# A nine-tap convolution computed with five products for three outputs instead of four for two

## What is computed

```python
sh = conv1d_same(xt, sh_w1, sh_b1)      # (B, 128, T) -> (B, 512, T), 9 taps
sh = jax.nn.silu(sh)
sh = conv1d_same(sh, sh_w2, sh_b2)      # 512 -> 128, 1 tap
...
z = residual + y + sh                   # y: the sum of the chosen experts
return (z - mu) * jax.lax.rsqrt(var + 1e-05) * ln_g + ln_b
```

## Time and profile before

| | us |
|---|---|
| median of 3 runs | 1534.27 |
| the profiled execution | 1544.43 |
| its span, first to last instruction | 1542.6 |
| TensorE busy (x10360 matmul records) | 1305.9 (85%) |
| VectorE busy | 1003.6 (65%) |
| GpSimd busy | 699.3 (45%) |
| ScalarE busy | 644.9 (42%) |
| convolution products (L1133), busy | 261.6, 1536 records |

### The profile page before, as it was taken

How to read it: one execution, slowest core, us unless ns; L and a number is a source line. 1 busy time by engine, 2 the same in 40 slices (tenths; PEclk the granted TensorE clock), 3 DMA queues, 4 the chain that set the end, 5 groups by cost and what they waited for, 6 DMA issues and landing times.

```text
span 1542.6 us, 33397 instructions
## 1 busy us (share of the span) xinstructions
PE 1305.9 (85%) x10360; PEld 1103.2 (72%) x10361; DVE 1003.6 (65%) x3235; ACT 644.9 (42%) x1610; POOL 699.3 (45%) x1055
## 2 busy tenths in 40 slices
PE   6696777787899937778899899988998989999974
PEld 3464646564899935556788778876887989999953
DVE  4467768665466656757863786467663628989946
ACT  1346272523122204335335453445334436666623
POOL 0112556444688853133531444242614526777732
PEclk9697989898999978989999899999998999999987
DMA  6000400003588840010010001000100237777725
GB/s 191 4 21 6 111 27 22 25 21 95 161 266 256 263 170 1 2 42 1 24 61 0 2 14 58 14 1 1 43 1 8 95 97 191 196 194 198 196 88 161
DMA packets 102202, 128.46 MB, mean 83 GB/s; under 512 B 21015, under 2 KB 61181, under 8 KB 101842
## 3 DMA queue, kind: packets, MB, share of 16 engines
q1 hardware_dynamic: 88786, 102.36, 23.1%
q0 software_dynamic: 13312, 24.74, 4.8%
HBM read 96.13 MB, written 34.94 MB: 85 GB/s over the span
## 4 chain that ended last, share of the span: by engine, by line
PE 60%; DVE 15%; issue 7%; DVEq 6%; POOL 5%; ACT 4%; DMA 2%; POOLq 0%; SPq 0%; ACTq 0%
PE psum L980 12%; PE psum L1133 11%; PE psum L989 9%; DVE work L1554 3%; PE psum L1142 3%; PE psum L1047 2%; POOL rows_in L2130 2%; PE psum L1094 2%; PE psum L1072 2%; PE psum L794 2%; PE psum L1191 2%; PE psum L969 2%; PE psum L1018 2%; DVE stats L1537 2%; PE psum L1067 1%
## 5 line engine op out<-in xcount | busy, mean ns | idle before, releaser
L1133 PE MATMUL psum<-NT,wreg 128*128 128x182 f32 (+1 forms) x1536 | 261.6, 326 | 10.2 <-ACT pack L1434 5.1
L1133 PEld LDWEIGHTS psum<-NT,wreg 128*128 128x128 f32 x1536 | 247.9, 192 | 18.9 <-ACT pack L1434 5.9
L2162 POOL DMA_INDIRECT rows_out<-work,expert_row_kept x208 | 206.2, 992 | 79.6 <-issue 41.1
L980 PE MATMUL psum<-work 128*128 128x128 f32 x1664 | 222.7, 277 | 0.9 <-ACT work L1336 0.9
L980 PEld LDWEIGHTS psum<-work 128*128 128x128 f32 x1664 | 203.9, 193 | 1.7 <-issue 0.9
L2111 POOL TENSOR_TENSOR rstd<-var_eps,pack 128x6 f32<-128x6 f32 x40 | 56.5, 1415 | 215.0 <-DVE var_eps L1544 214.9
L1329 ACT ACTIVATE work<-psum,work 128x128 f32<-128x128 f32 x416 | 118.6, 368 | 64.4 <-PE psum L980 64.3
L1876 DVE SCALAR_TENSOR_TENSOR work<-psum,work 128x128 f32<-128x128 f32 x416 | 117.1, 344 | 7.7
L794 PE MATMUL psum<-pack,work 128*128 128x128 f32 (+2 forms) x288 | 51.4, 336 | 82.0 <-DVE work L1554 75.5
L1885 DVE TENSOR_SCALAR work<-psum,expert_row_kept 128x128 f32<-128x128 f32 x208 | 72.8, 350 | 71.8 <-PE psum L969 36.6
L2130 POOL DMA_INDIRECT rows_in<-N,slot_now x96 | 100.5, 1046 | 28.6 <-issue 28.4
(11 more groups left out here) (364 smaller groups left out, 2894.3 us busy)
## 6 DMA issues: line engine op xcount, KB each, us to landing
work<-w_and_b SPq DMA_DIRECT2D x104, 258.0 KB
work<-in_ew SPq DMA_DIRECT2D x104, 256.0 KB
work<-rows_in SPq DMA_DIRECT2D x208, 65.0 KB
work<-rows_out SPq DMA_DIRECT2D x32, 384.0 KB, 4.2
rows_out<-work,expert_row_kept POOLq DMA_INDIRECT x208
work<-in_xT SPq DMA_DIRECT2D x8, 375.0 KB, 3.0
w_and_b<-in_ew SPq DMA_DIRECT2D x1, 2560.0 KB
out<-H SPq DMA_DIRECT2D x8, 320.0 KB
```

The lines of the kernel that those rows point to most:

```text
L980: r_ = mm(v.ps1[:, c * P:(c + 1) * P], v.w1[:, c * P:(c + 1) * P], v.xT, start=True, stop=True)
L1133: r = mm(bank[:, half * HALF_PAIRS:half * HALF_PAIRS + p1 - p0], weights[:, m * P:(m + 1) * P], product_input(name, g, k, p0, p1), start=( ...
L2162: G.indirect_dma_start(rows_out[m], bass.IndirectOffsetOnAxis(ap=v.dest, axis=0), v.y, None, bounds_check=last, oob_is_err=False).then_inc ...
```

## The change

The convolution now makes three outputs from five products (`CONV_POINTS`). A unit (k, m) is a whole sequence of lane k, 250 triples of outputs (`TRIPLES`), for 128 hidden features; there are 8 units per iteration. A unit has three parts: `p12` (6 products), `p03` (6) and `p4` (3). All parts, and `rows`, alternate between the two PSUM banks. Only `p12` has two SBUF buffers; `p03` and `p4` have one. VectorE combines with seven instructions. `turn` now has twelve GpSimd instructions in four steps with a drain between them. The weights of points 1, 2 and 3 are made by VectorE in the first iteration of the mixer, with five instructions over 1536 columns (`conv_w0` to `conv_w2`), stored to DRAM, and loaded when the first experts are done. Two of the four hidden blocks now lie in the first rows of `H`, which are saved to DRAM before and restored at the end.

```diff
-        FILL = [3, 1, 0, 0, 0, 0, 1, 0] + [0.5, 0.5] * TILES + [3.5, 2, 1.5, 1, 0.5]
+        FILL = [3, 1, 0, 0, 0, 0, 1, 0] + [0.5, 0.5] * TILES + [3.5, 2.5, 2, 1, 0]
...
+            for t in range(3):
+                sp.dma_start(raw_taps[:, t].rearrange("p (g c) -> p g c", g=3),
+                             d["conv1"].rearrange("p (g t c) -> p g t c", g=3, t=3)[:, :, t, :]).then_inc(conv_taps_in, 16)
...
+            sp.wait_ge(conv_made, 1)
+            sp.dma_start(conv_made_dram, raw_taps.rearrange("p t c -> p (t c)")).then_inc(conv_made_out, 16)
             with sp.Fori(1, ITERS) as i:
...
-            for name, dst in (("conv1", conv1), ("conv2", conv2)):
-                sp.dma_start(dst, d[name]).then_inc(conv_in, 16)
+            for t, x in ((0, 0), (2, 4)):
+                sp.dma_start(conv_w[:, x], d["conv1"].rearrange("p (g t c) -> p g t c", g=3, t=3)[:, :, t, :]).then_inc(conv_in, 16)
+            sp.dma_start(conv2, d["conv2"]).then_inc(conv_in, 16)
+            sp.wait_ge(conv_made_out, 16)
+            sp.dma_start(conv_w[:, 1:4].rearrange("p x g c -> p (x g c)"), conv_made_dram).then_inc(conv_in, 16)
...
+            sp.wait_ge(first_rows_final, 1)
+            sp.dma_start(first_rows_dram, first_rows).then_inc(first_rows_out, 16)
...
+            sp.dma_start(first_rows, first_rows_dram).then_inc(first_rows_back, 16)
...
+                    for half, x in enumerate(POINTS[what]):
                         for g in range(3):
+                            r = mm(bank[:, half * TRIPLES:(half + 1) * TRIPLES], conv_w[:, MADE[x], g, k_cols(m)], turned(k)[:, x, g:g + TRIPLES],
+                                   start=(g == 0), stop=(g == 2))
...
+                bk, bm, bi = unit_before(k, m, i, 2 if what == "p12" else 1)
+                e.wait_ge(dve_conv_done, dve_conv.at("conv", f"y{bm}_{bk}", 0, bi))
+                dst = {"p12": conv_p12[u % 2], "p03": conv_p03, "p4": conv_p4}[what]
...
-                V.tensor_tensor(conv_sum[:, 0:n_], b, c, ALU.add)
-                V.tensor_tensor(b, b, c, ALU.subtract)
+                V.scalar_tensor_tensor(conv_sum, p1, 3.0, p2, ALU.mult, ALU.add)
+                V.scalar_tensor_tensor(p2, p1, -3.0, p2, ALU.mult, ALU.add)
+                V.scalar_tensor_tensor(p0, p0, 3.0, p3, ALU.mult, ALU.add)
+                V.scalar_tensor_tensor(conv_p4, conv_p4, 1.5, p3, ALU.mult, ALU.add)
                 e.drain()
...
+                V.tensor_tensor(y[:, 0], p0, conv_sum, ALU.subtract)
+                V.scalar_tensor_tensor(y[:, 1], p3, 2.0, p2, ALU.mult, ALU.add)
+                V.scalar_tensor_tensor(y[:, 2], conv_p4, 4.0, conv_sum, ALU.mult, ALU.subtract
...
             def attention(i, first):
-                if not first:
-                    turn(1, i - 1)
...
                 turn(0, i)
+                for k in range(LANES):
+                    add_ln_b(k, i, first)
+                turn(1, i)
                 add_b_sh2(0, i)
```

More of the change, by code:

```diff
@@ L50 @@
 KTAPS = 9
+TRIPLES = (L + 2) // 3
+TURNED = TRIPLES + 2
 EPS = 1e-5
@@ L456, in run @@
                         continue
-                    if chain == "scatter":
+                    if chain == "conv_w":
+                        steps[step]()
+                    elif chain == "scatter":
                         steps[step](int(pair[0]) if pair else i - 2)
@@ L546, in audio_tower @@
         UNITS = 2 * LANES
-        HALF_PAIRS = SPAN[0][1] // 2
         pe_conv_done, act_conv_done, dve_conv_done = sem("pe_conv_done"), sem("act_conv_done"), sem("dve_conv_done")
-        UNIT = [(q, m) for q in range(UNITS) for m in range(4)]
+        UNIT = [(k, m) for k in range(LANES) for m in range(4)]
+        POINTS = {"p12": (1, 2), "p03": (0, 3), "p4": (4,)}
+        MADE = {0: 0, 1: 2, 2: 3, 3: 1, 4: 4}
         PARTS = []
-        for u, (q, m) in enumerate(UNIT):
-            PARTS.append(("bc", q, m))
-            if m == 1 and q > 0:
-                PARTS.append(("rows", q - 1, 0))
-            PARTS.append(("ad", q, m))
@@ L563, in audio_tower @@
-        dve_conv = Steps({"conv": (ITERS, 1, [f"y{m}_{q}" for q, m in UNIT])})
+        for k, m in UNIT:
+            PARTS.append(("p12", k, m))
+            if m == 1 and k > 0:
+                PARTS += [("rows", 2 * k - 2, 0), ("rows", 2 * k - 1, 0)]
+            PARTS += [("p03", k, m), ("p4", k, m)]
+        CONV_END = [("last", LANES - 1, 3), ("rows", UNITS - 2, 0), ("rows", UNITS - 1, 0)]
+        COST = {"p12": 6, "p03": 6, "p4": 3, "rows": 4}
+        FILLS = [f"{x}{m}_{k}" for x, k, m in PARTS + CONV_END if x != "last"]
@@ L584, in interleaved @@
                 reached += FILL[x // LANES]
-                while conv and n * sum(FILL) * LANES < reached * len(PARTS) and n < len(PARTS):
+                while conv and n < len(PARTS) and sum(costs[:n]) * sum(FILL) * LANES < reached * sum(costs):
                     order.append(("conv", n, 0))
@@ new lines, in conv_part @@
+                what, k, m = (PARTS + CONV_END)[n]
+                if what == "last":
+                    return
+                fill = f"{what}{m}_{k}"
+                bank = fill_bank(fill)
+                before, bi = fill_before(fill, i)
+                e.wait_ge(act_conv_done, act_conv.at("conv", before, 0, bi))
+                if what == "rows":
+                    q = k
+                    e.wait_ge(act_conv_done, act_conv.at("conv", f"s3_{q // 2}", 0, i))
+                    for j in range(3):
+                        tile = 3 * (q % 2) + j
+                        n_ = WIDTH[tile]
+                        for m in range(4):
+                            r = mm(bank[0:n_, j * P:(j + 1) * P], conv_h[m][:, tile * P:tile * P + n_], conv2[:, m * P:(m + 1) * P],
+                                   start=(m == 0), stop=(m == 3))
+                else:
+                    if what == "p12" and m == 0:
+                        e.wait_ge(pool_done[k], pool.at("attention", "turned", k, i))
+                    for half, x in enumerate(POINTS[what]):
+                        for g in range(3):
+                            r = mm(bank[:, half * TRIPLES:(half + 1) * TRIPLES], conv_w[:, MADE[x], g, k_cols(m)], turned(k)[:, x, g:g + TRIPLES],
+                                   start=(g == 0), stop=(g == 2))
@@ L1145, in none @@
+                r.then_inc(pe_conv_done, pe_conv.step("conv", fill, 0))
             def none(k, i):
@@ new lines, in conv_silu @@
+            def conv_silu(k, m, i):
+                e.wait_ge(dve_conv_done, dve_conv.at("conv", f"y{m}_{k}", 0, i))
+                A(conv_h[m][:, 0:L], conv_h[m][:, 0:L], ACT.Silu, bias=w("b_sh1", (m, m + 1)), scale=1.0 / 6.0
+                  ).then_inc(act_conv_done, act_conv.step("conv", f"s{m}_{k}", 0))
+            def conv_part(n, i):
+                what, k, m = (PARTS + CONV_END)[n]
+                u = 4 * k + m
+                if what == "last":
+                    conv_silu(k, m, i)
+                    return
+                fill = f"{what}{m}_{k}"
+                bank = fill_bank(fill)
+                e.wait_ge(pe_conv_done, pe_conv.at("conv", fill, 0, i))
+                if what == "rows":
+                    q = k
@@ L2260, in _ @@
                 attention(i, False)
-            turn(1, ITERS - 1)
             add_b_sh2(1, ITERS - 1)
```

246 lines of the change are left out of this document (127 added, 119 removed).

## The result

The median went from 1532.6 to 1554.1 us, the ratio is 1.0136 with an interval of 1.0075 to 1.0197. The forecast was 1536 with 1510 to 1550, and its likeliest case was no difference: the measured median lies above the range. The profiled execution of the changed kernel took 1549.0 us (span 1547.2) where the sum for a profiled one had said 1546.3. So the sum came close for the two executions that were profiled, by errors that cancel, and the step from there to the medians failed altogether. Later runs met five chips. Kernels are compared on one chip only. Three executions, one each of `fill_slots`, `mixer_after` and `combined`, took 64 to 700 us longer at a granted clock of 0.66 to 0.78 and are left out of the ratios.

A forecast was written before the change was run, and what follows sets the result against it. TensorE, busy 85% of the span, was taken to bound the kernel. The terms summed to +1.9, 1546.3 us for a profiled execution; as that one lay 10.2 above the median, the forecast was 1536, range 1510 to 1550.

The forecast's parts named there:

- Fewer products: Convolution on TensorE: 240 records of 250 columns, 50.4 us an iteration instead of 61.5; 9.9 less taken per loop iteration.
- The mixer, +8: Mixer's first iteration: VectorE's five instructions of 1536 columns delay the norms at two places, 8 us, bounds 0 to 10.
- The rival of late token loads: Mixer: token loads wait behind SP's wait for the weights' store; late by 5 us costs that once; part of a 0.08 case.
- Start of attention +3: More loads ahead of the sums of experts' rows, 4.19 MB instead of 2.62; 3 us later, between +2 and +6.
- making -7: GpSimd no longer makes wide weights, so a slow cycle of two lanes beside VectorE goes: 7 us saved.
- The first iteration's end, -2.4: End of the first iteration, which has no convolution: without a `turn` at the next start it saves 2.4 us.
- The meeting at the loop's end: GpSimd's `turn` holds VectorE's last combine; `rows` 49.8 us after attention's last output product; to `norm5T.1` +6.1, twice, then +9.8.
- The tail, -13: Tail after the loop: 68 us instead of 81.0, from shorter products, four `rows` of 11.2 and idle 5.5.
- From `norm5T.1` to T, -2.9: Up to attention's last output product (T): TensorE has 4.9 us less work, about 2 more idle; -2.9, three times.
- From the profile to the median: Last step: the profiled execution lay 10.2 us above the median, so 1546.3 for a profiled one became 1536.
- Rival B: Loop's end: the meeting costs little, 1511; halfway, each wait for one instruction only, 1529; chance with halfway 0.30.
- C: Loop's end, slower: `turn` takes 9.6 us and the second `rows` also runs at 1.2 GHz; 1549; chance 0.22.

The follow-up runs named there:

- fill_slots: Changed kernel with 1 instead of 0.5 for steps cx0 and sc1 in the table that places the convolution; 1541.0 us, ratio 1.0039 to the kernel before.
- mixer_after: Changed kernel with VectorE's five wide instructions all behind the mixer's first norms; ratio 0.9983 to the kernel before, on a 1655 us chip.
- combined: Changed kernel with lane 1's inputs later, fuller convolution table, last combine and SiLU ahead of scores, wide instructions behind first norms; ratio 0.9822 to the kernel before.
- late_turn: Changed kernel with lane 1's inputs (`turn`) moved to the next iteration, behind b_out's additions; 1557.9 us, ratio 1.0140 to the kernel before.
- turn_wide: Changed kernel with both turns as three back-to-back GpSimd instructions instead of twelve with three drains; `norm6T` to next `norm5T.1` 39.8 us, against 48.7 for the changed kernel.

## Where the prediction held and where it failed

**Fewer products: held.** 240 records in an iteration, 60 of them 12.4 us from the first start to the last, 0.21 each; the convolution's busy time went from 261.6 to 214.0.

**The mixer, +8: right where it acts.** The two places measured 3.5 and 3.5 us (idle 7.63 and 7.67 instead of 4.12), so +7. The first norms themselves came 2.2 us later and the second 5.5, since the products ahead of them were 1.3 us sooner in this execution, and 4.8 were left at the mixer's end. The rival of late token loads did not come.

**Start of attention +3, making -7: +2.0 and -9.3.** The first at its lower bound, the second better than said.

**The first iteration's end, -2.4: failed, it is +5.5.** The step said "without a `turn` at the next start it saves 2.4". `turn(1)` still stands ahead of the next `rstd5` on GpSimd, in 8.7 us instead of 4.3: the prediction counted a move past a queue's end as a removal. In the loop the scores' wait hides that; in the first iteration there is no convolution and nothing hides it. And `turn(0)` had GpSimd's pause of 8.64 us in its middle, which no row of the kernel before could have shown there. Either one is large enough to turn the loss into a gain: with `turn(1)` moved and the pause left, the stretch takes 40.3 us (`late_turn`); with `turn(1)` in its place, both turns short and the pause behind `turn(0)`, 39.8 (`turn_wide`); the kernel before has 43.6. The two were not separated further.

**The meeting at the loop's end: its mechanism was real, its price wrong.** T+49.8 was forecast for `rows`, T+44.3 came. The failing step is "four instructions are held in the four runs": GpSimd let one through after each of its instructions. The same holds for the meeting at `turn(0)`: unit 5's `y` came at T+17 and not at T+24, and TensorE did not stall. So the Trainium skill's rule ("SBUF — State Buffer", section "Who interferes with whom"), which the prediction set aside, describes these rows: 0.8 to 1.05 us beside instructions of 0.7 to 1.0. It does not describe L1916, which waited for a gap in the run (5.21 us, 3.23 with drains).

The trace that the prediction was read from had rows of both kinds inside the combine of before:

```profile
898.45 4.11 DVE L2015 TENSOR_TENSOR conv_sum<-conv_b_and_c 128x192 f32<-128x192 f32 x1
...
1012.36 1.70 DVE L2019 SCALAR_TENSOR_TENSOR conv_h<-conv_b_and_c,conv_a_and_d 128x182 f32<-128x182 f32 x1
```

Both take 0.35 us alone and met a run of GpSimd's additions; the first waited until the sixth was nearly over (902.3), with no gap in the run there, the second for one. So the size does not make the difference. In all 20 traces no SCALAR_TENSOR_TENSOR lasts past the start of a second instruction of GpSimd, and 30 TENSOR_TENSOR last past three or more; others of these pass after one (0.88 us for L2016 at 967.14). The new combine starts with four SCALAR_TENSOR_TENSOR. That points to the operation, but no run changed it alone, and what lets some TENSOR_TENSOR pass is open.

A second queue was overlooked: ScalarE's six copies stand ahead of that SiLU in the kernel before as well, and alone would have held `rows` to T+43.4 (an estimate: their end at 1022.7, and SiLU).

**The tail, -13: failed, it is -8.9.** It took 72.2 us where 68 were forecast and 81.0 stood before. The last two `rows` took 8.0 us instead of 5.6, since TensorE began them at 1.2 GHz after 5.0 us idle for the last combine; idle time was 7.4 instead of 6.3, the rest is small. It began at T+51.6 where T+58.1 was forecast, so the stretch from T on came out at -5.5 for -3.2, again by errors that cancel. The rival of a tail bound by the scatter did not come.

**From `norm5T.1` to T, -2.9: failed.** 97.5 us came where 92.8 were forecast. "About 2 more idle (fewer parts to fill with)" was a guess without a row; it was 6.2 more (from 4.8 to 11.0 us). The row to read was that of the `rows` part of 3.48 us beside VectorE's slots. With this and the meeting the errors are +4.7 and -4.3, so an iteration of 167.3 fitted the forecast of 167 for wrong reasons.

**The clock: missing, and the largest single term.** The prediction had it as a rival only for the second `rows`, which ran at the upper level. It was lost at `norm6T`, after 3.6 us of idle time that the kernel before does not have there (0.15), in some executions: 4.2 us per iteration, 12 in all.

**From the profile to the median: failed, and with it the forecast.** "That one is 10.2 above the median" took an offset from the kernel before to the changed one. About half or more of it was the start at 1.2 GHz, a matter of one execution; the changed kernel's median holds its own low stretches. 1546.3 became 1536. Of the 18.1 us by which the forecast missed, this step is 10.3; the profiled execution lay 2.7 above the sum, and the median 5.1 above the profiled execution. 1546.3 should have stayed, and with 12 for the clock in the loop it is 1558; the measured 1554.1 lies between.

Rival B, in its halfway form (each wait for one instruction only), had the mechanism of the meeting, but at 1529 it was priced without any of the losses beside it. C had the sign and nearly the size of the result (1549). Its first half came: `turn(1)` took 9.8 us. But `rows` did not wait for it, and the second `rows` ran at the upper level, so its number was luck.

## What to carry to other kernels

When work is taken from the engine that bounds, list each place where it had covered another engine's chain, and put the remaining parts there; here that, the last SiLU ahead of copies that nobody waits for, and two moves into idle time of GpSimd and VectorE turned 1.4% slower into 1.5% faster (on the 1655 us chips 0.3 to 0.6% slower into 1.8 to 2.4% faster). A wait seen in a profile has the last releaser's name only: before a term is priced, ask which other queue would be late right after it. And take more than one execution: the runs of one kernel on one chip differ by 16 to 18 us where nothing was edited, and a correction from one execution to the median belongs to that kernel alone.

## What the runs showed of the hardware

- TensorE's granted clock after the same idle time of 3.6 us differed between executions of one kernel, and between iterations of one execution: 1.2 or 2.4 GHz, 2.3 us apart on 18 records, 4 per iteration. At the start of the program it made 8.1 us at the first norms.
- A TENSOR_TENSOR of VectorE with both inputs in SBUF could wait past several of GpSimd's instructions, whatever its size: 5.21 us for two over 640 and 128 columns, and 4.11 us for one over 192 columns (0.36 alone). A drain in GpSimd's run ended the wait (3.23 us for the two). No SCALAR_TENSOR_TENSOR in the 20 traces was held past one instruction of GpSimd.
- GpSimd stood still for 8.64 us at the first drain of the first `turn(0)`, in 15 of 15 traces of kernels that have it, and 8.66 us behind `turn(0)` where this has no drain (`turn_wide`). The cause is not in the profile.
- Chips differ: the same kernel before took 1533 and 1536 us on two and 1653 to 1656 on three. Of the 108 us between two profiled executions, 31 lie in the first experts and 69 in attention (iterations of 163.7 and 187 to 189 us), where TensorE's idle time is put down to issue, 0.3 to 1.8 us at a time.
